# A one-core hybrid kernel: feed-forward in two halves with the expert shares loaded by DMA, and a prologue that runs the first batch's chain ahead

## The chip, the cores and the metric

The kernel runs on one core of a Trainium2 chip. The core has a matmul engine (TensorE, PE in the rows; its weight loads are listed apart as PEld), a vector engine (VectorE, DVE), an activation engine (ScalarE, ACT), a general engine (GpSimd, POOL) and SyncE (SP), which here does nothing but issue transfers. Five instruction streams run side by side and are held together by semaphores alone. The metric is the device time of one execution in microseconds, the median of the runs.

## The reference

The input is two sequences of 1024 tokens with 128 channels, float32. Four layers follow each other, each on the normalised rows, each added to its input:

```python
x = x + attention(layernorm(x))     # 16 heads of 8, softmax(q k' / sqrt(8) + bias[h, i - j]) v
x = x + ffn(layernorm(x))
x = x + x_n + mamba(x_n)            # x_n = layernorm(x): depthwise convolution, selective scan
x = x + ffn(layernorm(x))

def ffn(x):                         # 64 experts of hidden size 64, one shared expert of 256
    scores = sigmoid(x @ router_w.T)              # T x 64
    sfc = scores + correction_bias                # 8 groups of 8; the 4 groups with the best
    masked = where(group in top 4, sfc, 0)        #   sum of their two best experts stay
    tidx = top_k(masked, 8)
    tw = scores[tidx]; c = 2.5 * tw / (sum(tw) + 1e-20)
    routed = sum_e c[:, e, None] * (square(relu(x @ up_w[e])) @ down_w[e])
    return routed + square(relu(x @ shared_up_w)) @ shared_down_w
```

The bias of attention depends on the head and on the distance alone: a sum of 16 Gaussians, evaluated at 2047 distances. Every expert is computed for every token and weighted by c, which is zero for 56 of the 64. c is called the share of a token in an expert here.

## The kernel before, in words

Tokens lie in 16 tiles of 128 rows, four tiles make a quarter of 512 tokens, the columns of a matmul. A float32 product that needs precision is made of three matmuls of halves: the high half is the operand rounded to a shorter float (ACT copies it), the low half is what is left (POOL or DVE subtracts). Line numbers are those of the kernel before; after an arrow, of the changed one.

**Prologue of attention.** Rows are normalised batch by batch and turned (L1007), Q and K are projected (L1015) and split into three bf16 pieces: ACT takes the first (L1160), DVE subtracts it (L1234) and rounds the second (L1236), POOL subtracts the third (L963). SP stores the pieces to DRAM (L852), with all 128 partitions at once, and loads them back as stacks of heads (L878, L872). The bias is a matmul (L1037), copied by ACT and DVE, stored, and read back as two kinds of tables: `t_max` (L861, for the row maxima) and `t_col` (L866, for the scores).

**Main loop of attention.** 128 steps. In each, PE makes two pairs of row products into slots of PSUM (L1057); DVE adds the table and takes the maximum of each row (L1255, one slot at a time, both slots of a pair signalled by one semaphore). The first 22 pairs stand ahead of the first step. The maxima are negated, turned, and sent into the stack of Q by DMA, so that the scores (L1085) come out already less their maximum. ACT takes the exponential (L1203), PE multiplies by V (L1104).

**Feed-forward (`moe_ffn`).** All four quarters go together. First the head: normalise, turn, 32 tiles of logits (L354), sigmoid (L451), and on DVE the routing, in which groups and experts are ranked by comparisons over 16 tiles at a time (L524 to L567). c is written as two float16 pieces side by side and turned (L388) into `cT`. Then units. A unit is one pair of experts (2 x 64 hidden channels on 128 partitions) and one quarter: 8 shared ones first, then 32 x 4 routed ones. In a routed unit PE makes three up matmuls (L360 to L362), one matmul of `cT` with a matrix of ones and zeros, `spread` (L417), which puts each token's share of the two experts on their 64 partitions each, and, four units behind (LAG), three down matmuls into `acc` (L401). Between them ACT takes the relu (L478), DVE multiplies it by the share (L585) and by the unrectified product (L591), ACT rounds the result (L471) and POOL subtracts (L514). The weights of each pair are loaded in every stage (L320, L324) and split by ACT (L484) and DVE (L573), in two slots. At the end each quarter is turned back (L428) and added (L600); without an output, DVE takes the statistics for the next normalisation (L66).

The orders are written out by hand: each engine's block is a program of its own, and nothing is scheduled elsewhere. SP's and ACT's queues hold waits too; what stands behind a wait is issued after it.

## Time and profile before

| | us |
|---|---|
| median of 3 runs | 1184.79 (1184.17 to 1186.43) |
| the profiled execution | 1184.06 |
| its span in the trace | 1182.1 |
| PE busy | 1020.0 (86%) |
| DVE busy | 983.5 (83%) |
| ACT busy | 719.0 (61%) |
| POOL busy | 447.7 (38%) |
| POOL `f_act_low` (L514), 256 of them | 331.2 |
| PE `f_work` by `spread` (L417), 256 of them | 100.9 |

The span is that of the instructions; the 2.0 us that the execution takes beyond it lie around the program. Busy time is summed over an engine's instructions; matmuls overlap their neighbours, so the mean duration of one (394 ns for L417) is longer than the time between two of them. The share of busy time is a mean over stages with different limits. In names of tiles `f_` is the feed-forward (both stages), `at_` attention, `ss_` the state space. The page says of the chain that ended last: POOL 11% of the span, issue 9%, PE 1%; most of the span stands with no engine there.

### The profile page before, as it was taken

The page shows a single profiled execution, that of the slowest core. Times are in us where ns is not written, and L with a number is a line of the kernel's source. Part 1 is how long each engine was busy: PE and PEld are TensorE (multiplying, and loading weights), DVE is VectorE, ACT ScalarE, POOL GpSimd, SP SyncE. Part 2 cuts the span into 40 slices and gives each one's busy share as a digit, 9 for nine tenths or more (in the row PEclk, how much of TensorE's full clock was granted, in tenths as well). Part 3 has the DMA queues.
Part 4 walks back from the last instruction along what each step waited for, and adds up shares of the span by engine and source line. Part 5 has one row for each costly group of instructions (what it writes and reads, how often), then busy time and mean ns, then how long its engine had stood idle before and what let it go on. Part 6 is the DMA issues. An engine that isn't in the chain of part 4 may idle for free. (4 is left out here: it accounts for less than half of the span.)

```text
span 1182.1 us, 19693 instructions
## 1 busy us (share of the span) xinstructions
PE 1020.0 (86%) x5756; PEld 540.9 (46%) x5756; DVE 983.5 (83%) x2432; ACT 719.0 (61%) x1175; POOL 447.7 (38%) x404
## 2 busy tenths in 40 slices
PE   3559999999999999785999999782877769999998
PEld 1212222222222222264766676541656537666775
DVE  6589999889999986168999999787876689999997
ACT  5116665666666656564777777586333537777775
POOL 4600000000000000013777778515663127777776
PEclk9659999999999999967999999986889879999999
DMA  3740122032012200000000000000000000000001
GB/s 100 255 95 8 61 76 49 16 106 66 15 55 75 57 1 2 1 21 12 20 21 18 22 18 23 3 19 0 1 0 0 21 9 21 22 18 21 19 23 38
DMA packets 56704, 41.66 MB, mean 35 GB/s; under 512 B 23334, under 2 KB 51004, under 8 KB 56636
## 3 DMA queue, kind: packets, MB, share of 16 engines
q1 hardware_dynamic: 54268, 38.18, 12.0%
q10 hardware_dynamic: 2368, 2.63, 0.8%
q8 instruction: 36, 0.59, 0.2%
q14 instruction: 32, 0.26, 0.1%
HBM read 33.12 MB, written 7.47 MB: 34 GB/s over the span
## 5 line engine op out<-in xcount | busy, mean ns | idle before, releaser
L514 POOL TENSOR_TENSOR f_act_low<-f_act,f_act_high 128x512 fp32r<-128x512 f32 x256 | 331.2, 1294 | 151.3 <-ACT f_act_high L471 146.3
L1203 ACT ACTIVATE at_prob<-at_cols 128x1024 f32<-128x1024 f32 x256 | 248.1, 1021 | 198.4 <-PE at_cols L1092 198.4
L1255 DVE CUSTOM_DVE_ANT_0 at_rows<-at_rows,at_table_max 128x512 f32<-128x512 f32 x512 | 340.3, 719 | 33.5 <-PE at_rows L1057 32.3
L471 ACT CAST f_act_high<-f_act 128x512 fp32r<-128x512 f32 x256 | 159.1, 621 | 68.1 <-DVE f_act L591 65.7
L585 DVE TENSOR_TENSOR f_gated<-f_relu,f_work 128x512 f32<-128x512 f32 x256 | 174.3, 681 | 21.3 <-PE f_work L417 15.1
L591 DVE TENSOR_TENSOR f_act<-f_gated,f_work 128x512 f32<-128x512 f32 x256 | 175.8, 687 | 10.2
L478 ACT ACTIVATE f_relu<-f_work 128x512 f32<-128x512 f32 x256 | 152.9, 597 | 32.1 <-PE f_work L362 30.7
L360 PE MATMUL f_work<-f_x_high,f_wu_high 128*128 128x512 f32 x256 | 148.4, 580 | 2.7 <-DVE f_wu_low L573 2.1
L1057 PE MATMUL at_rows<-at_k_stack,at_q_stack 48*128 48x512 bf16 x512 | 104.7, 405 | 39.9 <-DVE at_maxima L1255 38.4
L1104 PE MATMUL at_pv<-at_prob,at_v_stack 128*32 128x512 f32 x1024 | 136.4, 605 | 0.6 <-ACT at_prob L1203 0.6
L1092 PE MATMUL at_cols<-at_table_cols,flip_sum 128*64 128x512 f16 x1024 | 136.4, 387 | 0.0
L979 POOL COPY at_v_stack<-at_v_nat 128x256 f32<-128x256 f32 x8 | 3.1, 400 | 333.1 <-PE at_pv L1104 333.1
L1057 PEld LDWEIGHTS at_rows<-at_k_stack,at_q_stack 48*128 48x128 bf16 x512 | 24.9, 93 | 189.2 <-DVE at_maxima L1255 150.1
L401 PE MATMUL f_acc<-f_act_high,f_wd_high 128*128 128x512 f32 x256 | 102.2, 399 | 2.4 <-POOL f_act_low L514 2.4
L417 PE MATMUL f_work<-f_cT,spread 128*128 128x512 f16 x256 | 100.9, 394 | 2.5 <-DVE f_gated L585 2.3
L361 PE MATMUL f_work<-f_x_low,f_wu_high 128*128 128x512 f32 x256 | 101.7, 397 | 0.0
L362 PE MATMUL f_work<-f_x_high,f_wu_low 128*128 128x512 f32 x256 | 101.6, 397 | 0.0
L401 PE MATMUL f_acc<-f_act_high,f_wd_low 128*128 128x512 f32 x256 | 101.5, 397 | 0.0
L401 PE MATMUL f_acc<-f_act_low,f_wd_high 128*128 128x512 f32 x256 | 101.5, 396 | 0.0
L1085 PE MATMUL at_cols<-at_q_stack,at_k_stack 51*128 51x512 bf16 x512 | 78.8, 379 | 2.6 <-ACT at_prob L1203 2.6
L1092 PEld LDWEIGHTS at_cols<-at_table_cols,flip_sum 128*64 128x64 f16 x1024 | 49.0, 109 | 63.7 <-issue 38.8
L1255 DVE DVE_READ_ACCUMULATOR2_ANT at_maxima<- 128x1 f32 x512 | 72.8, 142 | 0.0
(274 smaller groups left out, 1393.8 us busy)
## 6 DMA issues: line engine op xcount, KB each, us to landing
at_table_cols<-bias_rows SPq DMA_DIRECT2D x32, 248.0 KB, 5.1
at_table_max<-bias_rows SPq DMA_DIRECT2D x12, 480.0 KB, 4.3
f_wu<-in_L_ffn_up_w_dram SPq DMA_DIRECT2D x64, 64.0 KB, 2.0
f_wd<-in_L_ffn_down_w_dram SPq DMA_DIRECT2D x64, 64.0 KB, 1.8
at_q_stack<-q_parts SPq DMA_DIRECT2D x28, 96.0 KB, 2.4
at_k_stack<-k_parts SPq DMA_DIRECT2D x24, 96.0 KB, 3.9
at_table_max<-bias_rows ACTq DMA_DIRECT2D x4, 480.0 KB, 5.8
k_parts<-at_parts SPq DMA_DIRECT2D x2, 768.0 KB, 5.4
```

Source lines behind the costliest of these rows:

```text
L360: mm(hid[:, n % 3, :], w_hi, xh[:, cols], start=True, stop=False)
L401: last = mm(acc[:, j % 4, :], w[:, slot, :], x[:, j % 4, :], start=False, stop=(k == 2), skip_group_check=True)
L471: nc.scalar.copy(act_h[:, j % 4, :], act[:, j % 4, :]).then_inc(act_high, 1)
L478: nc.scalar.activation(relu[:, j % 2, :], hid[:, j % 3, :], ACT.Relu).then_inc(relu_ready, 1)
L514: nc.gpsimd.tensor_tensor(act_l[:, k, :], act[:, k, :], act_h[:, k, :].bitcast(F32), ALU.subtract).then_inc(act_low, 1)
L585: tt(gated[:, j % 2, :], relu[:, j % 2, :], cw, ALU.mult).then_inc(gate_done, 1)
L591: tt(act[:, j % 4, :], gated[:, j % 2, :], hid[:, j % 3, :], ALU.mult).then_inc(act_ready, 1)
L1057: last = mm(s1[:, (at + j) % SLOTS, :], q_st[r, p.b, p.lh, p.hp, p.lbq * P:(p.lbq + 1) * P], k_st[r, p.b, p.hp, p.mh * BANK:(p.mh + 1) * B ...
L1092: last = mm(s2[u * HALF:(u + 1) * HALF, hp, j, :], m.flip_sum[:], t_col[:, 2 * hp + j, c:c + BANK], start=False, stop=True)
L1104: last = mm(pv[32 * h:32 * h + 32, :], vst[:, it % 2, LT - 1 - s % LT, h, :], prob[:, S % 2, h, :], start=(s % LT == 0), stop=(s % LT == L ...
L1203: act(prob[:, S % 2, 2 * hp:2 * hp + 2, :], s2[:, hp, :, :], ACT.Exp).then_inc(exp_done, 1)
L1255: nc.vector.tensor_tensor_reduce(out=slot, in0=slot, in1=t_max[:, 2 * p.hp + j, c:c + BANK][:, ::-1], scale=1.0, scalar=-3.0e38, op0=ALU.a ...
```

## The change

**Prologue.** The first batch's chain comes first on every engine. DVE splits the first batch alone; ACT copies the second batch's projections whole and rounds them (L1312, L1313), POOL makes the rest (L1076 to L1080). SP stores only the 32 partitions of the first group of heads, loads K for it, and stores the other 96 behind. ACT stores half of the bias, and loads Q as well as the tables for the maxima. PE projects the second batch and its values between the pairs of maxima, and each matmul signals its own slot. The two rows of constants in the stack of K come by DMA.

Stores of SP in the prologue, before; `k_parts` and `q_parts` are the pieces in DRAM, `at_k_stack` what is loaded back:

```order
L852 DMA k_parts<-at_parts 128x3x1024
L852 DMA q_parts<-at_parts 128x3x1024
L852 DMA k_parts<-at_parts 128x2x1024
L852 DMA q_parts<-at_parts 128x2x1024
L852 DMA k_parts<-at_parts 128x1024
L852 DMA q_parts<-at_parts 128x1024
L878 DMA at_k_stack<-k_parts 48x2x1024 x2
```

and the same place now:

```order
L914 DMA k_parts<-at_parts 32x3x1024
L914 DMA q_parts<-at_parts 32x3x1024
L917 DMA bias_rows<-at_b_hi 16x512 x2
L914 DMA k_parts<-at_parts 32x2x1024
L914 DMA q_parts<-at_parts 32x2x1024
L914 DMA k_parts<-at_parts 32x1024
L914 DMA q_parts<-at_parts 32x1024
L952 DMA at_k_stack<-k_parts 48x2x1024 x2
L917 DMA bias_rows<-at_b_lo 16x512 x4
L914 DMA k_parts<-at_parts 96x3x1024
```

The stores shrink to a quarter of their partitions, and the bias has moved in between them, where it stood behind the second batch.

PE behind the bias matmul, before: `at_xn` is turned, values (L1024) and projections (L1015) follow, and only then the row products (L1057).

```order
L1007 MATMUL at_rows<-ident,at_xn 128x128 x4
L1007 MATMUL at_pv<-ident,at_xn 128x128 x4
L1024 MATMUL at_rows<-at_wT,at_xnT 128x128 x8
L1024 MATMUL at_pv<-at_wT,at_xnT 128x128 x4
L1024 MATMUL at_rows<-at_wT,at_xnT 128x128 x4
L1015 MATMUL at_cols<-at_xnT,at_wT 128x512 x4
L1057 MATMUL at_rows<-at_k_stack,at_q_stack 128x512 x36
```

Now (row products L1176, projections L1131, values L1160):

```order
L1126 MATMUL at_rows<-ident,at_xn 128x128 x8
L1176 MATMUL at_rows<-at_k_stack,at_q_stack 128x512 x4
L1131 MATMUL at_cols<-at_xnT,at_wT 128x512
L1176 MATMUL at_rows<-at_k_stack,at_q_stack 128x512 x2
L1131 MATMUL at_cols<-at_xnT,at_wT 128x512
L1176 MATMUL at_rows<-at_k_stack,at_q_stack 128x512 x2
L1131 MATMUL at_cols<-at_xnT,at_wT 128x512
L1176 MATMUL at_rows<-at_k_stack,at_q_stack 128x512 x2
L1131 MATMUL at_cols<-at_xnT,at_wT 128x512
L1176 MATMUL at_rows<-at_k_stack,at_q_stack 128x512 x2
L1160 MATMUL at_pv<-at_wT,at_xnT 128x128 x2
```

The row products have moved ahead, and the second batch's work stands between them.

**Feed-forward.** The weights of all 34 pairs are loaded once, during attention, split by POOL, and stay for both stages. A stage is done in two halves of 1024 tokens, 34 x 2 = 68 units each; the head of the second half (normalising to shares) is woven into the units of the first, and the tail of the first into the units of the second, at steps given in a table. The share comes in as its square root: DVE takes r = max(root of c, 1e-18), one Newton step (r' = (root + c / r) / 2), PE turns it, ACT copies it, and it is stored to DRAM; SP reads it back with two transfers for each pair of experts, one expert each, broadcast over 64 partitions, for both quarters. A unit then has six matmuls, one DVE instruction max(product, 0) x root share (L591), the square (ACT, L446), the rounding (L439) and the subtraction (POOL). `spread`, `cT` and the float16 pieces are gone.

In the state-space stage two sequences share one buffer for the convolution's input, and one buffer's name serves another; its order is as before.

PE in the first half of the first feed-forward stage, before:

```order
L360 MATMUL f1_work<-f1_x_high,f1_wu_high 128x512
L361 MATMUL f1_work<-f1_x_low,f1_wu_high 128x512
L362 MATMUL f1_work<-f1_x_high,f1_wu_low 128x512
L401 MATMUL f1_acc<-f1_act_high,f1_wd_high 128x512
L401 MATMUL f1_acc<-f1_act_low,f1_wd_high 128x512
L401 MATMUL f1_acc<-f1_act_high,f1_wd_low 128x512
L417 MATMUL f1_work<-f1_cT,spread 128x512
```

and now, at a step where the second half's rows are turned (`f1_hid` takes the up products, `f1_misc` the rest):

```order
L379 MATMUL f1_hid<-f1_x_high,wu_high 128x512
L379 MATMUL f1_hid<-f1_x_low,wu_high 128x512
L379 MATMUL f1_hid<-f1_x_high,wu_low 128x512
L386 MATMUL f1_acc<-f1_act_high,wd_high 128x512
L386 MATMUL f1_acc<-f1_act_low,wd_high 128x512
L386 MATMUL f1_acc<-f1_act_high,wd_low 128x512
L344 MATMUL f1_misc<-ident,f1_xn 128x128 x4
```

The spread matmul of each unit is gone. DVE, before, with the last routing instructions, the weight splits (L573) and the first routed units (L585, L591):

```order
L567 TENSOR_TENSOR f1_chl<-f1_struck,f1_chl 128x16x64
L569 COPY f1_cT<-f1_work 128x1024
L573 TENSOR_TENSOR f1_wu_low<-f1_wu,f1_wu_high 128x128 x2
L585 TENSOR_TENSOR f1_gated<-f1_relu,f1_work 128x512
L591 TENSOR_TENSOR f1_act<-f1_gated,f1_work 128x512
L585 TENSOR_TENSOR f1_gated<-f1_relu,f1_work 128x512
L591 TENSOR_TENSOR f1_act<-f1_gated,f1_work 128x512
L573 TENSOR_TENSOR f1_wd_low<-f1_wd,f1_wd_high 128x128
```

and now, where the second half is ranked (L523, L525) between units (L591):

```order
L591 SCALAR_TENSOR_TENSOR f1_gated<-f1_hid,f1_cw 128x512
L525 TENSOR_TENSOR f1_ahead<-f1_gsum 128x8x8
L523 TENSOR_TENSOR f1_ahead<-f1_gsum 128x8
L525 TENSOR_TENSOR f1_ahead<-f1_gsum 128x8x7
L591 SCALAR_TENSOR_TENSOR f1_gated<-f1_hid,f1_cw 128x512
L523 TENSOR_TENSOR f1_ahead<-f1_gsum 128x8x2
L525 TENSOR_TENSOR f1_ahead<-f1_gsum 128x8x6
```

One instruction per unit is left to DVE, and routing of 8 tiles at a time stands between them.

The diff, cut to its core (`-` lines are of before, `+` of now):

```diff
+NPAIRS = SHARED + PAIRS
+FFN_UNITS = NPAIRS * QH          # QH = 2 quarters of a half: 68
+C_SLOTS = 4; ACT_SLOTS = 4; PART_SLOTS = 6; LAG = 4
+def weave(main, side):            # side yields the step of main that its next piece stands behind
+    side = iter(side)
+    due = next(side, None)
+    for k, _ in enumerate(main):
+        while due is not None and due <= k + 1:
+            due = next(side, None)
+    ...
+AT_ROOT, AT_ROWS, AT_TURN, AT_COPY, AT_HIGH, AT_LOW, AT_LOGITS = 2, 3, 5, 6, 7, 8, 8
+AT_SCORE, AT_ROUTE = 12, 13
+AT_C_ROOT, AT_NEWTON, AT_C_TURN, AT_C_COPY = 38, 39, 42, 43
+AT_TAIL = 8
+        def stage_program(head, units, tail, eng):
+            run(head(eng, 0))
+            weave(units(eng, 0), head(eng, 1))
+            weave(units(eng, 1), tail(eng, 0))
+            run(tail(eng, 1))
+        def sp_shares(sp, b):
+            sp.wait_ge(h.rcT_ready, 1)
+            sp.dma_start(c_rows[QH * b:QH * (b + 1)].rearrange("q e t -> (q e) t"), rcT[:]).then_inc(h.rc_out, 16)
+            sp.wait_ge(h.rc_out, 16)
+            for k in range(PAIRS):
+                if k >= C_SLOTS:
+                    sp.wait_ge(h.gate_done, QH * (SHARED + k - C_SLOTS + 1))
+                ...
+                for e in range(2):
+                    src = c_rows[QH * b:QH * (b + 1), 2 * k + e, :].unsqueeze(0).broadcast_to([HID, QH, BANK])
+                    sp.dma_start(cw[HID * e:HID * (e + 1), (k + b * PAIRS) % C_SLOTS, :, :], src).then_inc(h.c_in[k % C_SLOTS], 16)
-                def unit(i, j):
-                    ...
-                    up(wu_h[:, slot, :], wu_l[:, slot, :], j % 4, j)
-                    if past(i, j, LAG):
-                        down_routed(i, j - LAG)
-                    if past(i, j, 1):
-                        pe.wait_ge(gate_done, BODY * i + j)
-                    mm(cw, m.spread[:, bass.ds(e, 2), :].rearrange("p e j -> p (e j)"),
-                       cT[:, (j % 4) * BANK:(j % 4 + 1) * BANK], start=True, stop=True).then_inc(cw_done, 1)
+            for n in range(FFN_UNITS + LAG):          # pe_units
+                if n < FFN_UNITS:
+                    up(n)                             # waits for gate_done n - 1: two banks
+                if n >= LAG:
+                    down(n - LAG)
+                yield
+                    k = n // QH - SHARED              # dve_units, a routed unit
+                    v.wait_ge(h.c_in[k % C_SLOTS], 32 * (k // C_SLOTS + 1))
+                    ins = nc.vector.scalar_tensor_tensor(out=gated[:, n % 3, :], in0=hid[:, n % 2, :], scalar=0.0,
+                                                         in1=cw[:, (k + b * PAIRS) % C_SLOTS, n % QH, :], op0=ALU.max, op1=ALU.mult)
+            nc.scalar.activation(root[:], masked[:], ACT.Sqrt).then_inc(h.root_ready, 1)
+            ch.link(ts(sfc[:], root[:], 1e-18, None, ALU.max))
+            ch.link(nc.vector.reciprocal(sfc[:], sfc[:]))
+            ch.link(tt(sfc[:], sfc[:], masked[:], ALU.mult))
+            ch.link(tt(sfc[:], sfc[:], root[:], ALU.add))
+            ts(rc[:]..., sfc[:]..., 0.5, None, ALU.mult).then_inc(h.rc_ready, 1)
 # attention
-            for n in range(KINDS // 2, KINDS):
-                split(n)                              # DVE, the second batch
+                for n in range(KINDS // 2, KINDS):    # POOL, the second batch
+                    tt(whole[:, n % 4, :], whole[:, n % 4, :], part(n, 0), ALU.subtract).then_inc(rest_ready, 1)
+                    nc.gpsimd.tensor_copy(part(n, 1), whole[:, n % 4, :]).then_inc(mid_ready, 1)
+                    tt(part(n, 2), whole[:, n % 4, :], part(n, 1), ALU.subtract).then_inc(low_ready, 1)
-                    if at + 2 > SLOTS:
-                        pe.wait_ge(slots_free, at + 2 - SLOTS)
                     for j in range(2):
+                        if at + j >= SLOTS:
+                            pe.wait_ge(slots_free, at + j + 1 - SLOTS)
-                    last.then_inc(fills, 1)
+                        mm(...).then_inc(fills, 1)
+                    if S in WEIGHT_STEPS:             # SP, steps 4, 16, 28, ...: 9 chunks of weights
+                        load_weights(sp, k)
+                    if S - 2 in WEIGHT_STEPS:         # POOL: two copies and two subtractions each
+                        split_weights(WEIGHT_STEPS.index(S - 2))
```

## Rows read from the trace of the kernel before

**Rows 1.** Windows: length; busy PE, PEld, DVE, ACT, POOL; clock, DMA share, GB/s.
```profile
0.00:80.90 80.90, 34.55 (x130) 15.60 (x132) 57.23 (x167) 19.39 (x24) 32.64 (x39) 0.72 0.56 164
80.90:499.00 418.10, 400.88 (x3107) 114.25 (x3103) 347.92 (x1101) 255.87 (x272) 2.40 (x6) 1.00 0.16 42
502.50:766.60 264.10, 241.65 (x1017) 169.67 (x1017) 231.50 (x452) 185.26 (x355) 171.24 (x133) 0.94 0.07 18
920.50:1182.10 261.60, 238.11 (x1017) 166.37 (x1017) 229.18 (x436) 184.12 (x354) 171.26 (x133) 0.95 0.08 22
```

**Rows 2.** Timeline of PE, one routed unit: start, us, engine, line.
```profile
1165.62 0.39 PE L417 MATMUL f_work<-f_cT,spread 128*128 128x512 f16 x1
...
1167.25 0.39 PE L417 MATMUL f_work<-f_cT,spread 128*128 128x512 f16 x1
```

**Rows 3.** Groups by line: busy us, mean ns of one, idle before.
```profile
L514 POOL TENSOR_TENSOR f_act_low<-f_act,f_act_high 128x512 fp32r<-128x512 f32 x256 | 331.2, 1294 | 151.3 <-ACT f_act_high L471 146.3
L471 ACT CAST f_act_high<-f_act 128x512 fp32r<-128x512 f32 x256 | 159.1, 621 | 68.1 <-DVE f_act L591 65.7
L585 DVE TENSOR_TENSOR f_gated<-f_relu,f_work 128x512 f32<-128x512 f32 x256 | 174.3, 681 | 21.3 <-PE f_work L417 15.1
...
L461 ACT ACTIVATE f_act<-f_relu 128x512 f32<-128x512 f32 x16 | 10.1, 632 | 0.5
```

**Rows 4.** Timeline, edges of the feed-forward stages: start, us.
```profile
509.83 6.92 PE L354 MATMUL f_work<-f_rwT,f_xnT 128*128 128x64 f32 x32
517.92 1.23 DVE L524 TENSOR_TENSOR f_sfc<-f_score,f_cbias 128x1024 f32<-128x1024 f32 x1 [9.37 <-ACT f_score L451]
539.66 0.69 DVE L566 CAST f_chl<-f_struck 128x1024 f16<-128x1024 f32 x1
544.63 0.77 PE L360 MATMUL f_work<-f_x_high,f_wu_high 128*128 128x512 f32 x1 [1.07 <-DVE f_wu_low L573]
759.63 0.39 PE L401 MATMUL f_acc<-f_act_high,f_wd_low 128*128 128x512 f32 x1
1177.47 1.42 DVE L600 TENSOR_TENSOR x_rows<-f_work,x_rows 128x512 f32<-128x512 f32 x2 [0.15 <-PE f_work L428]
```

**Rows 5.** Timeline of the prologue; last, the page's transfers: KB, us to landing.
```profile
41.37 0.69 DVE L1234 TENSOR_TENSOR at_rest<-at_cols,at_parts 128x512 f32<-128x512 f32 x1 [11.12 <-ACT at_parts L1160]
...
46.99 0.69 DVE L1255 CUSTOM_DVE_ANT_0 at_rows<-at_rows,at_table_max 128x512 f32<-128x512 f32 x1
...
48.44 0.70 DVE L1255 CUSTOM_DVE_ANT_0 at_rows<-at_rows,at_table_max 128x512 f32<-128x512 f32 x1
...
80.92 1.09 PE L1085 MATMUL at_cols<-at_q_stack,at_k_stack 51*128 51x512 bf16 x4
...
at_table_max<-bias_rows ACTq DMA_DIRECT2D x4, 480.0 KB, 5.8
```

**Rows 6.** Timeline, one pair of maxima in the main loop.
```profile
204.35 0.73 DVE L1255 CUSTOM_DVE_ANT_0 at_rows<-at_rows,at_table_max 128x512 f32<-128x512 f32 x1
...
205.65 0.73 DVE L1255 CUSTOM_DVE_ANT_0 at_rows<-at_rows,at_table_max 128x512 f32<-128x512 f32 x1
```

**Rows 7.** Timeline of POOL and DVE; last, one line's durations in ns, min/median/max.
```profile
549.40 2.66 POOL L514 TENSOR_TENSOR f_act_low<-f_act,f_act_high 128x512 fp32r<-128x512 f32 x2 [32.71 <-ACT f_act_high L471]
...
549.98 0.86 DVE L573 TENSOR_TENSOR f_wd_low<-f_wd,f_wd_high 128x128 fp32r<-128x128 f32 x1
...
L573 DVE TENSOR_TENSOR f_wu_low<-f_wu,f_wu_high x64: 281/627/819, 544.2 to 1160.9; 128x128 fp32r<-128x128 f32 x64
```

**Rows 8.** Groups by line: reciprocals, and a table load.
```profile
L1697 DVE RECIPROCAL ss_softplus<-ss_softplus 128x64 f32<-128x64 f32 x1 | 0.5, 547 | 0.0
L562 DVE RECIPROCAL f_wsum<-f_wsum 128x16 f32<-128x16 f32 x2 | 0.5, 252 | 0.1
L451 ACT ACT_TABLE_LOAD x2 | 2.6, 1283 | 0.0
```

**Rows 9.** Windows, while the tables are loaded.
```profile
65.00:70.00 5.00, 1.92 (x8) 0.41 (x8) 4.82 (x15) 0.00 (x0) 0.00 (x0) 0.50 1.11 235
```

1021 lines of the change are left out of this document (545 added, 476 removed).

## The prediction

> **What bounds the kernel now.** I read the clock and the busy time by stage first [rows 1]. The profiled execution takes 1184.06 us for a span of 1182.1 (2.0 lie around it), and the median of the three runs is 1184.79, so I work against the profiled execution and add 0.7 at the end. The rows show four pieces: a prologue up to 80.9 in which the matmul engine (PE) is busy for 34.6 of 80.9 us at a mean granted clock of 0.72; the main loop of attention, PE busy 400.9 of 418.1; and two feed-forward stages of 264.1 and 261.6 us with PE busy 241.7 and 238.1. The state-space stage between them is not touched in its order.
>
> Second, the timeline of one steady feed-forward unit [rows 2]: its spread matmul returns 1.63 us later, and seven matmuls of 512 columns fill that time, 0.2325 us each. PE is the bound there. Third, the groups by line [rows 3]: each unit costs POOL 1.294 for the subtraction, ACT 0.621 for the cast and about as much for the relu, DVE twice 0.681 or a little more. The reader is to see how close behind PE the POOL subtraction stands: 1.294 of 1.63.
>
> Fourth, the edges of the feed-forward stage [rows 4]: the stage begins at 502.5 [rows 1], the logits take 6.92 us, routing starts at 517.92 and reaches the f16 pieces of the shares at 539.66, the first routed matmul is at 544.63, the last at 759.63 + 0.39, and the stage ends at 766.6. So 42 us pass before routed work, in which PE has only the shared units to do.
>
> **Prologue.** DVE sits idle for 11.12 us before it splits the second batch, and its first row maximum starts only behind that, at 46.99; the first columns matmul follows at 80.92, after 22 pairs of maxima [rows 5]. After the change DVE splits only the first batch, POOL and ACT take the second, and PE projects the second batch between pairs. The first-batch chain then ends earlier: quarters 0 and 1 are normalised at about 11.4, DVE's four splits end at 24.4, the low half of the bias at 25, rows of the second batch at 29, its two transposed copies at 31. In parallel SP stores one head group of 32 partitions instead of 128, waits, and loads K near 31; ACT has the maximum tables behind bias stores that end near 28, plus the 5.8 us that their landing takes (last row of [rows 5]): 34. I take 35 for the first maximum, 12.0 us earlier; by the same rows it cannot be before 31 or (if ACT's queue holds the tables back, with its two DMA waits ahead of the loads) after 41. What is queued behind those waits on ACT is the second batch's copies, and PE waits for those, but only from pair 5 on.
>
> Each matmul now signals on its own and DVE waits slot by slot. At full supply four reductions take 1.30 us per pair, 204.35 to 205.65 [rows 6]; in the prologue a pair takes 1.45 (46.99 to 48.44), because both slots had to be free before PE refilled them at half clock. 22 pairs by 0.15 is 3.3; twelve of them now have a projection or two value matmuls between them, for which I take 0.3 back. Prologue: 12.0 + 3.3 - 0.3 = 15.0 us, bounds 7 and 20.
>
> **Main loop of attention.** I put it at 0. PE is busy 96% [rows 1]. POOL gets nine chunks of weights to split, at four instructions each, where it had 2.4 us of work in 418; DVE's reductions, 0.73 each [rows 6], read one operand from PSUM. If every one of the 36 held a reduction up by a tenth of a microsecond, the loss would be 3 us; I take that as its bound. A gain from the slot-wise signals is a rival below.
>
> **Feed-forward, steady.** The spread matmul goes: 6 x 0.2325 = 1.395 us per unit. Units are now 136 (8 shared ones with the same six matmuls). DVE has one instruction in place of two (0.69 by the product of 512, at most 0.1 more for its third operand), ACT 0.632 for the square, as the same form takes in the shared units, and 0.621 for the cast [rows 3]; the weight splits are gone. POOL, two instructions back to back in 2.66, needs 1.33 [rows 7]. So PE sets the pace and POOL is 0.07 behind it. A half of 68 units takes, from first down matmul to last, 67 x 1.395 + 0.70 = 94.2.
>
> **Feed-forward, edges.** A half starts with a fill: up 0.70, gate 0.75, square 0.63, the wait for the next unit's square 0.75, cast 0.62, subtraction 1.29 and about 0.8 of hand-overs, 5.6 in all, 6.0 when cold. There are now two per stage. Head of the first half: 8 tiles instead of 16. Of the 15.4 us to 517.92 go half of the logits (3.5) and about 0.85 of shorter rows: 11.0. Routing was 539.66 - 517.92 = 21.7 up to the f16 pieces; an instruction of 1024 elements takes 1.23 and one of 512 takes 0.681 [rows 3, 4], so 1.07 ns per element and 0.13 fixed; half the elements make about 13.3 with the small ones. Then the square root 0.65, clamp 0.6, reciprocal, two additions or products 1.44, scale 0.6, four transposes 1.1. The reciprocal of 512 elements is not in the trace; 16 take 0.252 and 64 take 0.547 [rows 8], 6.15 ns per element, so 3.3 (bounds: 0.7, as any other instruction, and 4.4, at the 8.5 ns that each of the 64 costs with its fixed part). Sum 32.1, before PE has anything else to do: routing is now bare. The weights' way to DRAM and back is about 6 us and lies beside the four shared units.
>
> Without interference: 32.1 + 6.0 + 94.2 + 5.6 + 94.2 + 1.1 (PE's transposes of half 0's output) + 2.9 (two quarters out, with statistics) = 236.1 against 264.1. In the last stage the square root's table is already loaded and the logits run warm: head 30.2, tail 2.0, 233.3 against 1177.47 + 1.42 - 920.5 = 258.4 [rows 4].
>
> **What the woven head costs.** The second half's head runs inside the first half's units, and this is the term that decides. While POOL subtracts, a DVE instruction with both inputs in SBUF stands still: the split at 549.98 needs 0.28 alone and took 0.86, ending 0.15 after the POOL instruction that began at 549.40; over the stage it has 0.281 least and 0.627 median [rows 7]. Most routing instructions are of that kind, and POOL now works 1.33 of every 1.395. A unit with s us of such work takes about 1.33 + s + 0.04. With s of 0.72, 0.80, 1.07, 1.09, four of 0.45, 0.72, 0.4 + 0.72, 0.72 and 0.45 + 0.72 the excess over 1.395 sums to 9. Around it: eight rows normalised in one block 1.3, the extra subtractions on POOL 0.5, a table load of 1.283 [rows 8] with the sigmoid 1.4 (ACT has 0.2 to spare per unit), the load, the root and the reciprocal behind it on DVE, ahead of the next gate, 4.8, the rest of that chain 1.5, PE's own transposes and logits 1.5. Together 20 us per stage. Bounds: 9 if the ports do not collide, 35 if every one of some 33 such instructions waits for a whole POOL instruction.
>
> [...]
>
> So the stages give 264.1 - 256.1 = 8.0 and 258.4 - 253.3 = 5.1.
>
> **Sum.** 15.0 + 0 + 8.0 + 5.1 = 28.1; 1184.06 - 28.1 = 1156.0, and on the median's scale 1156.7: 1157 us. With each term at its bound, and not all at once, the forecast case runs from 1140 (5 more gained in the prologue, some 11 more in one stage) to 1178 (8 fewer there, 13 fewer in the stages).
>
> **The shares by DMA.** Each pair of experts needs two transfers of 256 KB in 2 x 1.395 = 2.79 us, 188 GB/s, four slots deep. The nearest row is the window in which the table loads of 64 partitions run: 235 GB/s at a share of 1.11 [rows 9], so 212 at a full share, 2.5 us per pair. Hidden, with 0.3 us to spare and 8 us of depth for latency. [...]
>
> **The rivals.** (a) The ports collide little, or the woven work falls between POOL's instructions: the 9 and the 1.4 of the following additions go, 21 us over both stages, 1136. For it: the small DVE instructions are short. Against: the 0.627 median where POOL was busy only 79%. (b) The slot-wise signals remove PE's waits in the main loop. PE sits idle for 418.1 - 400.9 = 17.2 us there [rows 1]. At most some 15 of it can go, 1142. Against: PE still waits for the same second slot. (c) The prologue's chain is not ahead: the first maximum waits for the tables as before, only 3.3 remain, 1168. For it: three queues pass through one another's waits. (d) Slower: the shares set the pace. The gate waits for its slot on DVE, the matmuls two units behind it wait for the bank, and nothing catches up. It decides when a pair takes more than 2.79 us and eats the gain of 28 over 128 pairs at 3.01 us, that is under 174 GB/s. At 160 GB/s a pair takes 3.28, 0.49 x 128 = 62 more, of which some 17 lie in units already stretched: 1202. For it: broadcasts read one row of DRAM 64 times, the table loads do nearly the same and reach only 212. Against: those have packets of 992 bytes, these 2 KB.
>
> **How the numbers follow.** Forecast 0.45, (a) 0.14, (b) 0.10, (c) 0.13, (d) 0.18. The likeliest gives 1157. Case (d) lies above 1184 in most of its reach, and the forecast's worst corner adds nothing. Faster by over 0.2% (2.4 us, about what a measurement of this kernel tells from none): 0.81; within it 0.04, slower 0.15. The range leaves out the low corner of (a) with (b) and the upper half of (d): 1130 to 1192.
>
> **What would show it.** The first maximum near 35 and the first exponential near 68; a feed-forward unit of 1.40 us in the second half with PE without gaps; PE waiting on DVE or POOL in the routing units of the first half, DVE's two-input instructions stretched to over 1 us; the first shared matmul 32 us into the stage behind a reciprocal of over 3 us. DMA share near 0.9 and gates released by the DMA would show (d). The prediction is wrong if a steady unit is not 1.40, if the woven head costs under 10 or over 35 us a stage, or if the first maximum is not between 31 and 41.

## The result, and the profile after

The changed kernel takes 1157.68 us, the median of four runs (1157.08 to 1159.88), against 1184.88 of four runs of the kernel before on the same chip (1184.17 to 1186.43): ratio 0.9769, 95% interval 0.9751 to 0.9787. The forecast was 1157. The profiled execution took 1157.08, which is 26.98 less than the 1184.06 of before, where the prediction had 28.1.

That agreement of the total is partly luck. Stage by stage the account reads (us; a stage begins where the one above ends):

| stage | before | after | difference | predicted |
|---|---|---|---|---|
| start to first exponential of attention | 83.04 | 71.54 | -11.5 | -15.0 |
| from there to the first feed-forward stage | 419.53 | 423.53 | +4.0 | 0 |
| first feed-forward stage | 265.25 | 257.95 | -7.3 | -8.0 |
| state-space stage | 152.67 | 146.37 | -6.3 | 0 |
| second feed-forward stage | 261.61 | 255.91 | -5.7 | -5.1 |

The windows of the changed kernel for the same five stretches, with the columns of [rows 1]:

```profile
0.00:71.54 71.54, 44.26 (x145) 16.46 (x145) 52.68 (x164) 22.86 (x29) 24.24 (x41) 0.79 0.66 190
71.54:492.00 420.46, 407.71 (x3093) 116.31 (x3090) 350.14 (x1095) 255.87 (x272) 34.40 (x42) 0.99 0.20 51
495.07:753.02 257.95, 216.57 (x889) 165.04 (x889) 152.65 (x325) 168.33 (x294) 181.31 (x141) 0.91 0.49 133
753.02:899.39 146.37, 99.94 (x487) 70.48 (x487) 116.56 (x271) 73.53 (x169) 71.90 (x93) 0.87 0.02 4
899.39:1155.30 255.91, 215.50 (x889) 164.49 (x889) 149.52 (x308) 167.25 (x293) 181.47 (x140) 0.91 0.51 138
```

A feed-forward stage has 889 matmuls instead of 1017, PE is busy 25 us less in the first (23 in the second), and yet the stage is only 7 us shorter: PE now stands idle for 41 us of it, where it was 22. DMA carries 133 GB/s in it instead of 18.

The groups by line that answer to [rows 3], and the page's row of the shares' transfers (KB, us from issue to landing):

```profile
L475 POOL TENSOR_TENSOR f_act_low<-f_act,f_act_high 128x512 fp32r<-128x512 f32 x272 | 352.9, 1305 | 128.5 <-ACT f_act_high L439 112.7
L591 DVE SCALAR_TENSOR_TENSOR f_gated<-f_hid,f_cw 128x512 f32<-128x512 f32 x256 | 176.4, 690 | 155.2 <-PE f_hid L379 151.8
...
L568 DVE RECIPROCAL f_sfc<-f_sfc 128x512 f32<-128x512 f32 x4 | 13.4, 3353 | 0.1
...
f_cw<-f_c_rows SPq DMA_DIRECT2D x256, 256.0 KB, 4.4
```

The gate waits for PE (151.8 of 155.2 us) and not for its share from the DMA: rival (d) has no row. The third operand costs DVE 9 ns (690 for 681). In steady units the gates follow each other 1.39 or 1.40 us apart, 1.398 in the mean.

The prologue, with the columns of [rows 5]: first row products, first maximum, first projection of the second batch, first columns, and the first exponential behind a table load:

```profile
34.70 1.01 PE L1176 MATMUL at_rows<-at_k_stack,at_q_stack 48*128 48x512 bf16 x3 [5.19 <-DMA at_q_stack<-q_parts]
35.44 0.70 DVE L1380 CUSTOM_DVE_ANT_0 at_rows<-at_rows,at_table_max 128x512 f32<-128x512 f32 x1 [5.21 <-PE at_rows L1176]
36.79 2.07 PE L1131 MATMUL at_cols<-at_xnT,at_wT 128*128 128x512 f32 x2
67.71 1.45 PE L1203 MATMUL at_cols<-at_q_stack,at_k_stack 51*128 51x512 bf16 x4
70.25 1.28 ACT L1332 ACT_TABLE_LOAD   x1 [15.30 <-PE at_cols L1210]
71.54 1.94 ACT L1332 ACTIVATE at_prob<-at_cols 128x1024 f32<-128x1024 f32 x2
```

The first maximum is at 35.44 (forecast 35, before 46.99). The 22 pairs behind it took 32.27 us against 33.93 before, so they brought 1.7 and not 3.0. The two pairs that hold the first projections take 2.73 and 2.50 us, most of the others 1.30 as forecast: PE works at half clock there, and its two projection matmuls last 2.07 us (third row). From the first columns to the first exponential it is 3.83 us where it was 2.12: the exponential's table is loaded late (1.28), because the root in the second batch's norm had changed it, and the columns took 1.45 instead of 1.09.

The rows of a feed-forward stage's second half are normalised between the first half's units (timeline, DVE and POOL):

```profile
531.78 2.51 POOL L475 TENSOR_TENSOR f_act_low<-f_act,f_act_high 128x512 fp32r<-128x512 f32 x2 [28.74 <-ACT f_act_high L439]
532.09 3.83 DVE L792 TENSOR_SCALAR f_xn<-x_rows,f_tmp 128x128 f32<-128x128 f32 x8
537.76 2.52 POOL L475 TENSOR_TENSOR f_act_low<-f_act,f_act_high 128x512 fp32r<-128x512 f32 x2 [3.47 <-ACT f_act_high L439]
```

Eight rows that took 2.14 us in a block of the bare head (496.81) take 3.83 here, the gate waits behind them, and POOL then waits 3.47. From the first subtraction, 531.78, to the last of the half, 646.10, are 114.32 us for 67 steps of 1.398: 20.6 more than 93.7 (forecast 20). In the second stage the same half takes 112.9, 19.3 more. The head without cover took 31.6 us to its first matmul (forecast 32.1), and 31.4 in the second stage (forecast 30.2): the granted clock was 0.50 there too, from 899.39 to 930, so the logits did not run warm as forecast.

### The profile page after: what moved, and what is told of

It is laid out like the page before. It is cut to its first block and busy times, and to the rows that moved or that the text cites. A ratio compares the mean times of both kernels' runs of the same rounds, so it can differ in the third digit from the quotient of the medians.

```text
span 1155.3 us, 16936 instructions
## 1 busy us (share of the span) xinstructions
PE 984.0 (85%) x5500; PEld 532.8 (46%) x5500; DVE 823.1 (71%) x2168; ACT 687.9 (60%) x1057; POOL 493.3 (43%) x456
## 3 DMA queue, kind: packets, MB, share of 16 engines
HBM read 95.77 MB, written 8.52 MB: 90 GB/s over the span
## 5 line engine op out<-in xcount | busy, mean ns | idle before, releaser
L591 DVE SCALAR_TENSOR_TENSOR f_gated<-f_hid,f_cw 128x512 f32<-128x512 f32 x256 | 176.4, 690 | 155.2 <-PE f_hid L379 151.8
L446 ACT ACTIVATE f_act<-f_gated 128x512 f32<-128x512 f32 x272 | 172.0, 632 | 112.7 <-DVE f_gated L591 91.1
L439 ACT CAST f_act_high<-f_act 128x512 fp32r<-128x512 f32 x272 | 164.1, 605 | 0.0
L1176 PE MATMUL at_rows<-at_k_stack,at_q_stack 48*128 48x512 bf16 x512 | 119.1, 398 | 18.2 <-DVE at_maxima L1380 12.5
L379 PE MATMUL f_hid<-f_x_high,wu_high 128*128 128x512 f32 x272 | 115.9, 426 | 15.3 <-DVE f_gated L591 12.7
L386 PE MATMUL f_acc<-f_act_high,wd_high 128*128 128x512 f32 x272 | 112.9, 415 | 8.1 <-POOL f_act_low L475 7.9
L1176 PEld LDWEIGHTS at_rows<-at_k_stack,at_q_stack 48*128 48x128 bf16 x512 | 29.0, 93 | 177.2 <-DVE at_maxima L1380 120.3
L379 PE MATMUL f_hid<-f_x_high,wu_low 128*128 128x512 f32 x272 | 109.9, 404 | 0.0
L379 PE MATMUL f_hid<-f_x_low,wu_high 128*128 128x512 f32 x272 | 109.1, 401 | 0.0
L386 PE MATMUL f_acc<-f_act_low,wd_high 128*128 128x512 f32 x272 | 108.8, 400 | 0.0
L386 PE MATMUL f_acc<-f_act_high,wd_low 128*128 128x512 f32 x272 | 108.2, 398 | 0.0
L379 PEld LDWEIGHTS f_hid<-f_x_high,wu_high 128*128 128x128 f32 x272 | 52.9, 195 | 38.7 <-DVE f_gated L591 21.8
L386 PEld LDWEIGHTS f_acc<-f_act_high,wd_high 128*128 128x128 f32 x272 | 51.6, 190 | 34.0 <-POOL f_act_low L475 23.9
## 6 DMA issues: line engine op xcount, KB each, us to landing
f_cw<-f_c_rows SPq DMA_DIRECT2D x256, 256.0 KB, 4.4
at_raw_weights<-in_L_ffn_up_w_dram SPq DMA_DIRECT2D x8, 256.0 KB, 4.3
at_raw_weights<-in_L_ffn_down_w_dram SPq DMA_DIRECT2D x8, 256.0 KB, 4.8
```

Source lines behind the costliest of these rows:

```text
L379: last = nc.tensor.matmul(hid[:, n % 2, :], w[:, pp, :], x[:, cols], start=(k == 0), stop=(k == 2))
L386: last = nc.tensor.matmul(acc[:, QH * b + n % QH, :], w[:, pp, :], x[:, s, :], start=(pp == 0 and k == 0), stop=(pp == NPAIRS - 1 and k == 2),
L439: nc.scalar.copy(act_h[:, n % PART_SLOTS, :], act[:, n % ACT_SLOTS, :]).then_inc(h.high_done, 1)
L446: nc.scalar.activation(act[:, n % ACT_SLOTS, :], gated[:, n % 3, :], ACT.Square).then_inc(h.square_done, 1)
L591: ins = nc.vector.scalar_tensor_tensor(out=gated[:, n % 3, :], in0=hid[:, n % 2, :], scalar=0.0, in1=cw[:, (k + b * PAIRS) % C_SLOTS, n % ...
L1176: mm(s1[:, (at + j) % SLOTS, :], q_st[r, p.b, p.lh, p.hp, p.lbq * P:(p.lbq + 1) * P], k_st[r, p.b, p.hp, p.mh * BANK:(p.mh + 1) * BANK], s ...
```

## The experiments

Each row is a kernel of its own; "span" is that of the profiled execution, the other columns the stages of the table above (attention: when the first feed-forward stage begins).

| kernel | median us | ratio to before | span | attention | first ff | state space | second ff |
|---|---|---|---|---|---|---|---|
| before | 1184.88 | 1 | 1182.1 | 502.6 | 265.2 | 152.7 | 261.6 |
| after | 1157.68 | 0.9769 [0.9751, 0.9787] | 1155.3 | 495.1 | 257.9 | 146.4 | 255.9 |
| mamba_only | 1187.20 | 1.0012 [0.9998, 1.0026] | 1182.2 | 502.3 | 265.2 | 153.4 | 261.4 |
| mamba_moved | 1186.45 | 1.0014 [1.0004, 1.0023] | 1184.3 | 504.4 | 265.3 | 153.4 | 261.2 |
| scan_warm | 1195.00 | 1.0091 [1.0075, 1.0106] | 1192.7 | 503.1 | 265.3 | 162.7 | 261.6 |
| slotwise_only | 1181.98 | 0.9965 [0.9951, 0.9979] | 1180.0 | 500.3 | 265.2 | 151.3 | 263.2 |
| unwoven | 1179.70 | 0.9950 [0.9934, 0.9967] | 1175.1 | 496.4 | 266.6 | 146.4 | 265.7 |
| pool_short | 1135.19 | 0.9578 [0.9551, 0.9605] | 1133.5 | 496.7 | 245.1 | 145.9 | 245.8 |
| in_pieces | 1150.55 | 0.9694 [0.9675, 0.9713] | 1148.7 | 495.4 | 254.0 | 147.4 | 252.0 |
| shares_twice | 1366.57 | 1.1502 [1.1464, 1.1540] | 1367.4 | 495.0 | 358.6 | 150.6 | 363.2 |
| shares_once | 1157.69 | 0.9793 [0.9767, 0.9818] | 1150.4 | 492.3 | 256.0 | 146.2 | 255.9 |
| weights_between | 1157.87 | 0.9762 [0.9741, 0.9783] | 1153.7 | 494.0 | 258.3 | 145.5 | 255.9 |
| kept_warm | 1158.17 | 0.9760 [0.9737, 0.9782] | 1156.3 | 497.7 | 256.3 | 146.4 | 255.9 |
| pieces_and_weights | 1146.72 | 0.9677 [0.9663, 0.9690] | 1140.5 | 493.0 | 251.2 | 145.6 | 250.7 |

The ratios are paired with runs of the kernel before beside each kernel. The kernels were measured on two chips, with medians of 1184.33 to 1186.65 for the kernel before, so medians of two kernels that lie within about 2 us are to be compared by their ratios.

**pool_short: what the woven head costs.** POOL's subtraction is cut to 64 of 512 columns; the low halves' other 448 columns stay zero, so it leaves work out and shows only what POOL's share of the time does.

```diff
-                nc.gpsimd.tensor_tensor(act_l[:, n % PART_SLOTS, :], act[:, n % ACT_SLOTS, :],
+                nc.gpsimd.tensor_tensor(act_l[:, n % PART_SLOTS, 0:64], act[:, n % ACT_SLOTS, 0:64],
```

> The changed kernel in which POOL subtracts only 64 of the 512 columns of each routed and shared unit, so the low half of the other columns stays zero: POOL is busy for about 0.2 of every 1.4 us. Theory P (collisions with POOL stretch the woven routing): the stretched instructions return to their bare durations (rank threshold 0.20 instead of 1.24, f_struck 0.69 instead of 1.46, eight rows in 2.1 instead of 3.8 us), and the woven first half falls by about 7 us per stage, from 114.3 to about 107; the units without routing stay at 1.40 since PE sets them. Fill shorter by 1.1 in each half. Total about 1157.7 - 2 x (7 + 2) = 1140. Rival Q: the cost is the order of work on DVE and ACT (blocks ahead of the gate, the table load), then the woven half stays above 112 and only the fills gain, total 1152 to 1155.

Measured: 22.5 us less than after, 12.8 and 10.1 in the two stages. The collision holds, and is somewhat larger than the 7 us expected: the woven half shrinks from 114.32 to 102.98 in the first stage and from 112.9 to 103.8 in the second, 0.9 of which is the last, shorter subtraction. Of the first stage's 10.4 us that are left, about 1.9 go with the clock, as the comparison with shares_once below shows; so POOL costs about 8.5 of the 20.6 us, and 8.2 in the second stage. DVE's busy time in the woven half falls by 8.9 us (74.2 to 65.3), with the same instructions. Not all of the 8.5 need be that: behind a delay the units catch up at 1.25 us apiece beside a full POOL and at 1.04 beside a short one, and no run separates the two.

The durations of three DVE instructions with and without a busy POOL (ns, least/median/most), first of the changed kernel:

```profile
L792 DVE TENSOR_SCALAR f_xn<-x_rows,f_tmp x32: 332/338/1318, 496.8 to 939.7; 128x128 f32<-128x128 f32 x32
L532 DVE TENSOR_SCALAR f_rank<-f_rank x4: 195/719/1243, 512.1 to 971.2; 128x64 f32<-128x64 f32 x4
L551 DVE TENSOR_TENSOR f_struck<-f_struck,f_masked x4: 691/1071/1459, 515.9 to 980.3; 128x512 f32<-128x512 f32 x4
```

and the same of pool_short:

```profile
L796 DVE TENSOR_SCALAR f_xn<-x_rows,f_tmp x32: 333/340/347, 500.1 to 928.2; 128x128 f32<-128x128 f32 x32
L536 DVE TENSOR_SCALAR f_rank<-f_rank x4: 194/195/195, 515.4 to 956.0; 128x64 f32<-128x64 f32 x4
L555 DVE TENSOR_TENSOR f_struck<-f_struck,f_masked x4: 691/692/692, 519.2 to 964.1; 128x512 f32<-128x512 f32 x4
```

With POOL short, least and most lie within 14 ns. Instructions with one SBUF tensor (the first two) wait as those with two do (the third). The page "SBUF — State Buffer" of the Trainium skill, section "Who interferes with whom", has this too: `tensor_scalar`, copy and cast can enter a two-port mode and then take the pair that GpSimd reads through. My prediction put a price only on instructions with both inputs in SBUF. The other half of the 20.6 is there without POOL: in pool_short the unit behind the block of rows still takes 3.16 us, the one with the table load and root 2.98, the one with the reciprocal 4.72 and the next 2.04, which together is 7.3 us over four steady units.

**unwoven: does weaving pay at all?** The second half's head runs bare, ahead of the first half's units.

```diff
             run(head(eng, 0))
-            weave(units(eng, 0), head(eng, 1))
+            run(head(eng, 1))
+            run(units(eng, 0))
```

> The changed kernel with the second half's head run before the first half's units instead of inside them; nothing is left out. Bare, a head takes about 31.6 us (495.07 to 526.7 in the changed kernel); woven, it costs 20.6 us less the fill (531.78 to 646.10 for 67 units at 1.398 us, 93.7). Theory: weaving hides about a third of the head, so each of the two stages becomes 8 to 12 us longer and the kernel takes 1174 to 1181. Rival: the woven instructions cost more than they hide, then it is no slower than 1160. Steady units stay at 1.40 us and the first half then takes 94 us from first to last subtraction.

Measured: the stages are 8.7 and 9.8 us longer than in after. The head costs about 29 us bare and 20 woven, so weaving hides only a third of it.

**in_pieces: the same work in smaller bites.** Two rows per unit instead of eight, the reciprocal in four, and the steps of the table behind them moved to later units.

```diff
+            for t in range(0, HT, 2):
+                norms[b].vector_rows(v, b * HT + t, 2)
+                yield AT_ROWS + t // 2 + 1
...
+            for t in range(0, HT, 2):
+                ch.link(nc.vector.reciprocal(sfc[:, t:t + 2, :], sfc[:, t:t + 2, :]))
+                yield AT_NEWTON + t // 2 + 1
```

> The changed kernel with the woven head spread: the eight rows normalised two per unit instead of in one block, the reciprocal of 512 elements as four of 128, and the steps behind them moved (turning at 7, logits at 10, sigmoid at 14, routing from 16, square root at 41, Newton from 43, turning the shares at 50). In the changed kernel the units at these two places take 4.73 us (rows) and 3.04 + 4.72 + 2.05 us (root and reciprocal) where 1.40 is the pace: 3.3 and 5.6 us above it. Theory B (blocks ahead of the gate cost what they take beyond a unit's slack of 0.7 us): rows keep about 1, the reciprocal and root about 1.5, so 5 to 6 us per stage less, total 1146 to 1148. Rival C (every SBUF instruction waits for POOL, pieces wait more often): under 2 us per stage, total 1154 or more. The bare head of the first half becomes about 0.3 us longer by the pieces' fixed part.

Measured: 3.9 and 4.0 us per stage, under the 5 to 6 expected. What is left shows in DVE's timeline: the product and the sum stand together ahead of one gate, and each waits out a subtraction (0.68 alone), so that this unit takes 3.93 us from gate to gate:

```profile
607.10 1.60 DVE L573 TENSOR_TENSOR f_sfc<-f_sfc,f_masked 128x512 f32<-128x512 f32 x1
608.74 1.65 DVE L574 TENSOR_TENSOR f_sfc<-f_sfc,f_root 128x512 f32<-128x512 f32 x1
610.42 0.69 DVE L594 SCALAR_TENSOR_TENSOR f_gated<-f_hid,f_cw 128x512 f32<-128x512 f32 x1
```

**shares_twice and shares_once: the transfers.** One doubles every transfer (into a second buffer that nobody reads); the other issues only the first four pairs' transfers and uses those shares for all, leaving the others out.

```diff
 # shares_twice
                     sp.dma_start(cw[...], src).then_inc(h.c_in[k % C_SLOTS], 16)
+                    sp.dma_start(cw2[...], src).then_inc(h.c_in[k % C_SLOTS], 16)
 # shares_once
-                for e in range(2):
+                for e in range(2 if k < C_SLOTS else 0):
```

> The changed kernel with every transfer of shares issued twice, the second one into a buffer that nobody reads; the gate waits for both. It doubles the demand to 1 MB per pair of units, 376 GB/s at the full pace. Prediction's rate: 235 GB/s at a share of 1.11, 212 at a full share. Theory D: the transfers then set the pace, a pair of units takes 1048576 / 212 GB/s = 4.9 us instead of 2.79, the two stages grow by 2.15 x 128 = 275 us less what the stretched units hide, total about 1400 to 1435, and the rate read off is the limit against which the 188 GB/s of the changed kernel stand. Rival: the queue moves broadcasts at more than 300 GB/s, then a pair takes under 3.5 us and the total is under 1250.

> The changed kernel in which only the first four pairs of experts of each half have their shares loaded; the others reuse them (the shares of later pairs are left out). The transfers of the other 112 of 128 pairs go. Issuing each twice gave 4.68 us for 1 MB, 224 GB/s, so a pair's 512 KB take 2.34 of 2.79 us. Theory H (hidden): units without routing stay at 1.40 and the total is 1155 to 1158.5. Rival D2 (the transfers hold some gates up in the woven half, where catching up runs at 1.27 us a unit and would need 2.54 us per pair): 2 to 6 us faster, in the first halves.

Doubled, the transfers set the pace: 367.4 of the 378.3 us that DVE stands idle before its gates are put down to the share's DMA, and none in after. A steady stretch of shares_twice, with the columns of [rows 1]:

```profile
760.00:790.00 30.00, 21.77 (x80) 13.57 (x78) 7.73 (x12) 13.94 (x26) 17.18 (x14) 1.00 1.07 226
```

and one of the changed kernel:

```profile
680.00:710.00 30.00, 30.00 (x130) 24.20 (x129) 14.92 (x22) 24.43 (x44) 27.90 (x23) 1.00 0.65 188
```

With doubled transfers a pair of units took 4.68 us for 1 MB, 224 GB/s. Other stretches of shares_twice, 30 and 40 us long at a share of 1.06 to 1.08, lie between 214 and 226, so 512 KB need 2.32 to 2.45 of the 2.79 us that the units take, at the 188 GB/s in the second row. The margin is 0.3 to 0.5 us; the prediction had 0.3, but by dividing a rate by a share above 1, which by the same rule would make 211 of the 226 here.

Without the transfers the second stage is as long as with them (255.9 each). The first is 1.9 shorter; 1.6 of that lie in its first two routed units, and go with the clock. The same three microseconds, in after and then in shares_once:

```profile
536.50:539.50 3.00, 2.93 (x8) 2.25 (x9) 1.90 (x4) 2.77 (x6) 1.74 (x2) 0.53 1.08 229
```

```profile
533.70:536.70 3.00, 2.88 (x14) 2.31 (x15) 1.99 (x5) 2.90 (x6) 1.68 (x2) 1.00 1.06 228
```

PE does 8 matmuls at a granted clock of 0.53 in the one and 14 at 1.00 in the other, and the transfers run in both (these shares are still loaded in shares_once). So the transfers are hidden, and rival (d) falls; D2's 2 to 6 us are not there either.

**slotwise_only: rival (b).** The kernel before with nothing but the slot-wise signals.

```diff
-                    v.wait_ge(fills, slots.filled["pair", n])
...
+                        v.wait_ge(fills, at + j + 1)
+                        if at + j >= SLOTS:
+                            pe.wait_ge(slots_free, at + j + 1 - SLOTS)
```

> The kernel before with the slot-wise signals alone: each row matmul signals its own slot, PE and DVE wait slot by slot. By the prediction's term 22 pairs in the prologue run at 1.30 in place of 1.45 us: 3.3 us less, first columns near 77.6, total about 1181.5. Rival (b) of the prediction: PE's waits in the main loop go too, up to 15 us: the 128 steps take 398 to 405 instead of 412.5 us between first and last exponential. Rival N: nothing changes (DVE's reductions set the pace either way), within 1 us of 1184.8.

Measured: the first exponential is 4.25 us earlier (I had 3.3 for 22 pairs), four steps later the lead is 2.03, and it stays at 2.0 to 2.3 to the end of attention. Rival (b) falls: the signals bring nothing in the main loop. What took half of the gain back goes with the clock. Windows of slotwise_only at the start of the loop:

```profile
80.00:84.00 4.00, 3.58 (x16) 0.83 (x13) 2.70 (x8) 1.25 (x2) 0.00 (x0) 0.50 0.00 0
84.00:88.00 4.00, 4.00 (x28) 0.98 (x26) 2.81 (x8) 1.84 (x3) 0.00 (x0) 0.80 0.00 0
```

PE starts the loop earlier and does its first steps at a granted 0.50, that is at 1.2 GHz. In the kernel before the clock was at 0.50 too until just ahead of the loop (78 to 83), but at 0.87 in its first four microseconds (83 to 87).

**kept_warm: filling PE's gaps.** Matmuls whose result is not used stand ahead of the first pair and behind each of the late ones.

```diff
+                for _ in range(2):
+                    mm(proj_bank(3), wT[:, 1, :], xnT[:, 0:BANK], start=True, stop=True)
...
+                    if n > KINDS // 2 + 2 * NQ:
+                        mm(proj_bank(3)[:, 0:2 * P], wT[:, 1, :], xnT[:, 0:2 * P], start=True, stop=True)
```

> The changed kernel with extra matmuls whose result nobody reads: two of 512 columns ahead of the first pair of maxima, where PE waits 5.19 us for the loads, and one of 256 columns behind each of the pairs 17 to 21. In the changed kernel PE works at 0.50 of its clock from 34.7 to about 42 and again from about 59 to 79, and the lead over the kernel before shrinks by 2.1 us between the first exponential and step 4. Theory K (the clock costs it): PE comes to the projections between the pairs at the full clock, the first columns come 2 to 3 us earlier than 67.71, and the 2.1 us at the loop's start shrink to under 1; attention 3 to 5 us shorter, total 1153 to 1155. Rival: the pairs' pace is DVE's and the extra matmuls delay the real ones: no change or up to 2 us slower.

Measured: no gain, and the first exponential at 73.83, 2.3 later than after. Its trace around the fall of the clock (PE's timeline; the wait for DVE stands at the row's end):

```profile
59.01 0.70 PE L1238 MATMUL at_cols<-at_xnT,at_wT 128*128 128x256 f32 x2
...
61.27 0.39 PE L1176 MATMUL at_rows<-at_k_stack,at_q_stack 48*128 48x512 bf16 x1 [1.24 <-DVE at_maxima L1386]
...
63.75 1.22 PE L1238 MATMUL at_cols<-at_xnT,at_wT 128*128 128x256 f32 x2
```

PE still waited once for 1.24 us, the clock fell at about 63 all the same (granted 1.00 from 62 to 63 and 0.53 from 63 to 64), and the filler itself then took 1.22 per two instead of 0.70 and held the pairs up.

**weights_between: the losses inside the loop.** The changed kernel's lead over before, by the start of the same exponential, was 11.50 at the first, 9.41 at step 4, 9.44 at step 16, 8.52 at 20, 8.64 at 76, 7.37 at 80 and 7.17 at the last, 127. So there are four losses: 2.1 at the start and 0.9, 1.3 and 0.3 further on. The last three lie where POOL splits a chunk of weights (timeline of after; the third row is who waits, the sum itself in the first group and PE in the second):

```profile
131.14 0.29 DVE L1418 TENSOR_TENSOR at_onorm<-at_rows,at_rden 128x128 f32<-128x128 f32 x1
131.27 1.27 POOL L1106 TENSOR_TENSOR wd_low<-at_raw_weights,wd_high 128x512 fp32r<-128x512 f32 x1
131.46 1.23 DVE L1422 TENSOR_TENSOR x_rows<-x_rows,at_onorm 128x128 f32<-128x128 f32 x1
...
324.53 1.29 POOL L1106 TENSOR_TENSOR wu_low<-at_raw_weights,wu_high 128x512 fp32r<-128x512 f32 x1
324.73 1.13 DVE L1400 CAST at_negm<-at_mtop 128x16 bf16<-128x16 f32 x1
...
326.57 0.39 PE L1176 MATMUL at_rows<-at_k_stack,at_q_stack 48*128 48x512 bf16 x1 [1.66 <-DVE at_maxima L1380]
```

A sum that needs 0.29 takes 1.23, and a cast of 16 elements that needs 0.17 takes 1.13. weights_between loads the chunks eight steps apart and holds the split back until two steps later.

```diff
-WEIGHT_STEPS = tuple(4 + 12 * k for k in range(1 + PAIRS // WPAIRS))
+WEIGHT_STEPS = tuple(4 + 8 * k for k in range(1 + PAIRS // WPAIRS))
...
+                    pool.wait_ge(exp_done, 2 * (WEIGHT_STEPS[k] + 2))
```

> The changed kernel with the weight chunks loaded every 8 steps instead of every 12, and their split on POOL released only when the step after the negation of the maxima has its exponential, so that POOL's two copies and two subtractions lie between steps 6 and 9 of each 8, where DVE has only reductions. In the changed kernel the lead over the kernel before fell by 0.92 us at steps 16 to 20, by 1.27 at steps 76 to 80 and by 0.26 at steps 88 to 92; the rows there show a sum x_rows of 1.23 us instead of 0.29 and a cast of the negated maxima of 1.13 us instead of about 0.2, each beside a POOL subtraction of 1.28. Theory W (collisions with the splits): these three losses go, attention 2.2 to 2.5 us shorter, total 1155.4. Rival: the losses come from the transfers of the weights, then they stay near steps 4 to 76, total 1157 to 1158.

Measured: the lead is 8.12 at step 4 and 8.13 to 8.26 to the end; the three losses are gone. They are gone in pieces_and_weights too, while the seven kernels that split as after does lose 1.9 to 3.7 us between step 16 and the last. The two instructions now never vary (ns, least/median/most):

```profile
L1423 DVE TENSOR_TENSOR x_rows<-x_rows,at_onorm x16: 291/292/295, 106.8 to 491.3; 128x128 f32<-128x128 f32 x16
L1401 DVE CAST at_negm<-at_mtop x16: 174/174/176, 61.2 to 456.6; 128x16 bf16<-128x16 f32 x16
```

The total can nevertheless not be told from that of after (ratio 0.9762 against 0.9769, with intervals that overlap): in this execution the first exponential stood at 72.59, 1.05 later, so the loop began with that much less.

**The clock at the start of the loop, by an accident of shares_once.** Its attention is the same program as that of after, and its clock rose earlier. Windows of after:

```profile
70.00:74.00 4.00, 3.47 (x14) 0.57 (x10) 2.41 (x7) 3.22 (x3) 1.29 (x3) 0.50 0.00 0
74.00:78.00 4.00, 4.00 (x20) 0.86 (x18) 1.69 (x6) 1.94 (x2) 0.90 (x2) 0.50 0.01 2
78.00:82.00 4.00, 4.00 (x30) 1.02 (x28) 2.47 (x7) 1.81 (x2) 0.00 (x0) 0.84 0.00 0
```

and of shares_once:

```profile
66.00:70.00 4.00, 3.87 (x15) 0.95 (x14) 2.70 (x10) 0.64 (x1) 0.00 (x0) 0.50 0.19 49
70.00:74.00 4.00, 2.96 (x20) 0.82 (x18) 2.70 (x8) 2.95 (x4) 2.10 (x4) 0.90 0.01 2
74.00:78.00 4.00, 4.00 (x36) 1.03 (x34) 3.29 (x9) 2.88 (x4) 0.09 (x1) 1.00 0.00 0
```

The four steps from the first exponential took 14.77 us in after and 12.16 in shares_once: 2.6 us go with the moment at which the clock rises, and one program has both. Four more kernels here have this attention program (pool_short, unwoven, in_pieces, shares_twice): in these the four steps took 14.5 to 15.1, and over all six the first exponential stood between 70.65 and 73.07. So a change worth 1 us in attention is not to be read from a single span. No run sets the clock by itself, so that it costs the 2 us is argued from these traces and not shown by an experiment.

**mamba_only, mamba_moved, scan_warm: the 6.3 us of the state-space stage.** The first two make the edits of that stage in the kernel before (one buffer shared by two sequences, one name for another), the second with the stage's buffers at the addresses that they have in after; the third gives PE 34 unused matmuls ahead of the scan. (The first two also have the wait on ACT that the shared buffer needs.)

```diff
 # mamba_only
-        raw = sb("raw", [P, CB, SEQS, SEQ + CONV - 1])
+        raw = sb("raw", [P, CB, SEQ + CONV - 1])
-        yg = sb("yg", [P, NT, INNER])
+        yg = sz
 # mamba_moved: the same, and
+        sb("room", [P, 15296])
 # scan_warm
+                for _ in range(34):
+                    mm(ps[:, 0, :], wx[:, 0, :], xnT[:, 0:BANK], start=True, stop=True)
```

> The kernel before with only the state-space edit (one convolution buffer shared by both sequences, with the extra wait on ACT; yg under the name sz). In the changed kernel that stage took 146.4 us (753.02 to 899.39) against 152.7 (767.82 to 920.49) before. Theory S1: the edit itself brings it, by another pattern of work on PE and a higher granted clock in the scan. Then this kernel is 5 to 7 us faster than before, about 1178.5, with a stage of about 146.4. Rival S2: the stage depends on when it starts or on what ran before it, and the edit is worth nothing or costs the 3 us by which the projections became longer. Then 1184 to 1188 and a stage of 152 to 156.

> The kernel of mamba_only (before, with the state-space edit) with 61184 bytes per partition left free ahead of the stage's tiles, which puts them at the addresses that they have in the changed kernel, where the resident weights lie there (69632 bytes, less the 8448 of the constants that went). Theory M (the place of the tiles in SBUF makes the stage faster): stage 146 to 147, total 1178. Rival: it stays at 153, total 1184 to 1187; then what is left is the moment and the clock at which the stage starts.

> The kernel before with 34 extra matmuls of 512 columns, whose result nobody reads, in the 20 us in which PE waits between the projections of the state space and its scan. In the kernel before PE starts the scan at 0.50 of its clock and has 0.98 only 8 us later, falls to 0.78 and 0.58 in between; in the changed one, whose scan is the same program, the clock stays at 1.00 through the second and third step. Theory G (the clock at the start sets the pattern of the scan): the scan starts at the full clock, the stage falls from 152.7 to 145 to 149, total 1178 to 1181. Rival: the clock is a consequence of the pattern between DVE and POOL, the stage loses at most 2 us.

All three theories fell; S2 and the rival of mamba_moved came out. The window of the stage in mamba_only:

```profile
767.50:920.80 153.30, 103.09 (x487) 73.53 (x487) 115.82 (x271) 74.74 (x170) 69.03 (x93) 0.86 0.02 4
```

It takes 153.3 us, and 153.4 in mamba_moved, no better than before. In scan_warm the scan did start at full clock, but behind the filler, and from 831.87 to its end at 931.1 it took 99.3 us, against 97.3 before (823.21 to 920.49) and 90.0 after (809.40 to 899.39):

```profile
829.00:833.00 4.00, 3.07 (x16) 1.97 (x15) 0.96 (x4) 1.36 (x3) 1.54 (x2) 1.00 0.00 0
```

A cold start of the scan is not it, though its clock fell to 0.72 again from 837 to 841. Where in the stage the 6.3 us lie can be read: up to the scan the changed kernel takes 1.0 us more (56.4 for 55.4), from there to the end 7.3 less. In the scan POOL's product ss_R and DVE's product ss_M fall beside each other in one of two patterns that repeat every two steps. POOL's timeline of before:

```profile
865.36 1.22 POOL L1645 TENSOR_TENSOR ss_R<-upto,ss_dec 128x512 f32<-128x512 f32 x1
867.11 1.22 POOL L1645 TENSOR_TENSOR ss_R<-upto,ss_dec 128x512 f32<-128x512 f32 x1
```

and of after:

```profile
849.60 1.04 POOL L1772 TENSOR_TENSOR ss_R<-upto,ss_dec 128x512 f32<-128x512 f32 x1
851.35 1.49 POOL L1772 TENSOR_TENSOR ss_R<-upto,ss_dec 128x512 f32<-128x512 f32 x1
```

With 1.22 and 1.22 two steps take 9.27 us at the least, with 1.04 and 1.49 they take 8.75. The kernel before and the four built from it have the first pattern for most of the scan, after and the eight built from it the second; shares_twice leaves it for four of its sixteen ss_R, and its stage, 150.6, is the longest of these nine (4.2 us over after, 1.4 of them in the scan). From the first ss_R to the last it is 65.9 us before, 64.1 in mamba_only and 61.0 after, so 3 to 5 of the 7.3 us lie there. So the two kernels differ in how DVE and POOL get in each other's way, which the prediction put at nothing here. What puts a kernel into the one pattern or the other stays open. Over all runs the stage took 151.3 to 153.4 us in kernels built from before (scan_warm aside) and 145.5 to 150.6 in those built from after, with one and the same program in the latter.

**pieces_and_weights: the best of it together.** in_pieces with product, sum and scale in separate units, and weights_between.

```diff
             ch.link(tt(sfc[:], sfc[:], masked[:], ALU.mult))
+            yield AT_NEWTON + 6
             ch.link(tt(sfc[:], sfc[:], root[:], ALU.add))
-            yield AT_NEWTON + 2
+            yield AT_NEWTON + 8
```

> The changed kernel with the pieces of in_pieces, the product and the sum of the Newton step set two units apart from each other (in in_pieces they stand together ahead of one gate, take 1.60 and 1.65 us beside POOL, and that unit takes 3.93 us), and the weight splits of weights_between. From in_pieces (1150.5): the two units give 1.3 to 1.6 us per stage, the splits 1 to 2.2 in attention. Theory: 1145 to 1148, each feed-forward stage 250 to 253 us. Rival: apart, each of the two still waits for a POOL instruction and nothing is won, 1149 to 1150.

Measured: 1146.72, ratio 0.9677 [0.9663, 0.9690], against 0.9769 [0.9751, 0.9787] of after: faster by about 11 us. Against in_pieces (0.9694 [0.9675, 0.9713]) the intervals overlap, so the step beyond it is read from the stages alone, 2.8 and 1.3 us shorter. Its timeline where in_pieces had both together:

```profile
604.80 1.60 DVE L573 TENSOR_TENSOR f_sfc<-f_sfc,f_masked 128x512 f32<-128x512 f32 x1
606.44 1.29 DVE L595 SCALAR_TENSOR_TENSOR f_gated<-f_hid,f_cw 128x512 f32<-128x512 f32 x2
607.64 0.68 DVE L575 TENSOR_TENSOR f_sfc<-f_sfc,f_root 128x512 f32<-128x512 f32 x1
```

The two units take 2.25 and 1.85 instead of one of 3.93 and a steady one, and the stages 251.2 and 250.7.

## Why the prediction was right, point by point

- **First maximum 12.0 us earlier: right** (11.55, at 35.44). The order in which three queues pass through one another's waits was read correctly, and rival (c) falls.
- **Slot-wise signals, 3.3 less 0.3: the term was mis-sized, in both directions.** Alone they take 4.4 us off the 22 pairs (slotwise_only, 29.5 for 33.9). The work between the pairs takes 2.8 back and not 0.3, nearly all of it in two pairs where PE does two projection matmuls in 2.07 us at half clock. And I gave nothing for the table load of 1.28 ahead of the first exponential and the slower columns, 1.7 together. 11.55 + 4.4 - 2.8 - 1.7 is the measured prologue of 11.5, instead of 15.0.
- **Main loop 0, at most 3: wrong by 4.0 us.** 2.1 are lost in the first four steps, where PE stays at 1.2 GHz for some 6 us longer than before; that the clock takes them is argued, not shown. 2.2 go to POOL's splits (0.9, 1.3 and 0.3, less what comes back between them), and 0.3 come back behind the last exponential. The step that failed is the one where I looked only at the reductions, which read PSUM and are indeed free (719 ns each, before and after). The instructions behind them, a cast of 16 elements and the sum into x_rows, wait while POOL subtracts (1.13 for 0.17 and 1.23 for 0.29). That the three losses and both waits go with weights_between shows it.
- **Steady unit 1.395: right** (1.40), with the DMA at 188 GB/s beside it.
- **Routing bare, 32.1: right** (31.6), and the reciprocal's 3.3, extrapolated from [rows 8], measured 3.353.
- **Woven head 20: right in total (20.6 and 19.3), and not in its parts.** I had 9 for the ports, 10.4 in rival (a)'s price; pool_short gives about 8.5. Near, but by another sum: part of it is the rows' block (3.83 for 2.14) and other `tensor_scalar` instructions, which I had left out of the collision. Rival (a)'s price of 21 us over both stages is close to what a short POOL gives (22.9 measured, with shorter fills and 1.9 of clock in it), but POOL is in the way.
- **Stages -8.0 and -5.1: right** (-7.3 and -5.7). The second's head was put 1.9 below the first's, for a loaded table and warm logits, and measured only 0.2 below it (31.4 and 31.6).
- **State-space stage 0: wrong by 6.3 us, and not explained.** The step that failed is "not touched in its order": a stage whose order is the same need not take the same time. The traces show a second pattern between DVE and POOL in its scan, but not why it sets in. Without it the kernel would have measured about 1164, still in the range and the same case, 7 us over the forecast. The closeness of the total is owed to this.
- **(d):** the transfers need 2.3 to 2.45 of 2.79 us, the prediction had 2.5. The Trainium skill, page "SBUF — State Buffer", gives about 196 GB/s over partitions 0 to 63 (section "Door 1: The DMA port swizzle") and 6% more for a second transfer on the other half (section "Can I just issue two DMAs to hit both halves?"), by which a pair would take an estimated 2.5 to 2.7 us. The measured 214 to 226 GB/s is faster, and the measurement decides.

## What to carry to other kernels

When work is woven into a loop, price every instruction on DVE by whether GpSimd reads SBUF beside it, the tiny ones too, cut long blocks into pieces, and put at most one such piece ahead of each gate where it can be done: the same work cost 5 to 7 us per stage less in that form (pieces_and_weights). When a chain is moved earlier, ask at what clock the engine then enters the loop; the lead at its first step is not the lead that it keeps. And add up a forecast stage by stage: a total that fits may hold two errors of opposite sign.

## What the runs showed of the hardware that I had not expected

- A DVE cast of 128x16, 0.174 us alone, took up to 1.13 beside a POOL subtraction, a `tensor_scalar` of 128x64 1.24 for 0.195. Each came up to about 1 us late, whatever its size: the longest durations, less the shortest, are 0.77 to 1.05 us for DVE instructions of 16 to 512 columns, under the 1.27 to 1.30 of one subtraction.
- One attention program was at a granted clock of 0.90 from 70 to 74 us in one execution and at 0.50 until 78 in another, 2.6 us apart over four steps. A single wait of 1.24 us in an otherwise filled PE stood just before a fall of the clock.
- The state-space stage runs in 145.5 to 153.4 us depending on the kernel around it (scan_warm, with its filler, aside), with the same instructions in mamba_only (153.4) as in after (146.4). In the two kernels that tried them, neither its buffers' addresses nor the clock at the scan's start made the difference. DVE and POOL run in one of two patterns there, 9.27 or 8.75 us per two steps at the least, and shares_twice changes between them within one scan.
